# Moving the last 128 columns of each attention tile's polynomial from VectorE to GpSimd in an eight-core attention and feed-forward kernel

## The chip, the cores and the metric

One Trainium2 chip; the program runs on all 8 of its cores, with different data and the same instructions. The metric is device time in microseconds (us) of the slowest core. The engines of a core are TensorE (PE in the profile, its weight loads PEld), VectorE (DVE), ScalarE (ACT), GpSimd (POOL) and SyncE (SP, which issues most of the DMAs).

## The reference

One transformer layer on x of shape (4, 4096, 1024), float32. Cut to what matters:

```python
def polymax(x):                       # in place of a softmax
    poly = where(x > 0, x ** 2 + 1.0, 0.0)
    lin  = where((x >= -100) & (x <= 0), -0.01 * x + 1.0, 0.0)
    return (poly + lin) / 1000.0

def attn(x, W_attn, W_proj):          # 16 heads of 64, causal
    q, k, v = split(x @ W_attn)
    att = einsum('bhid,bhjd->bhij', q, k) / 8
    att = polymax(where(causal, att, -inf))
    return einsum('bhij,bhjd->bhid', att, v) @ W_proj

def ffn(x, U1, V1, b1, U2, V2, b2):   # low rank, 256
    return gelu(x @ U1 @ V1 + b1) @ U2 @ V2 + b2

x = x + attn(layernorm(x), W_attn, W_proj)
x = x + ffn(layernorm(x), U1, V1, b1, U2, V2, b2)
```

## The kernel before

**Split over cores.** Two cores share one of the four sequences. Each core computes keys and values of all 4096 positions and attention, projection and feed-forward for 2048 of them (every second tile of 128 rows). Data lie transposed: features on the 128 partitions, positions along the free dimension.

**Stages, one after the other.** (1) Layernorm of the whole sequence. (2) K, V and Q projections for the first half of the keys, and running sums of k times v (`msnap`, `prefsnap`). (3) Attention over the first half of the keys, `emit_attention(0)`. (4) K and V of the second half. (5) `emit_attention(1)`. (6) Projection, second layernorm, feed-forward, output. A bf16 score s is turned into relu(s) times (relu(s) + 0.01): with the linear part taken from the running sums, that is polymax up to constants.

**Attention, the part that is touched.** The loops are: chunk c (four query chunks of 512 columns), head pair p (8), key tile idx (up to 16 tiles of 128 keys). I call one (c, p) a sweep. One key tile of one head pair goes through five steps, in buffer `sb = idx % 3` of three:

- QK, L688 (`emit_qk`): two TensorE matmuls, one for each head, into two PSUM banks, N columns each. N is 512, but for the last six key tiles of a chunk's diagonal it is 384, 384, 256, 256, 128, 128.
- relu, L708: ScalarE reads both banks (2 x N columns) and writes `eb`. Masked tiles (eight for each chunk, those on the diagonal) have a second ScalarE operation, L713, on the first 128 columns of each head, into `zb`.
- polynomial, L721: VectorE, one SCALAR_TENSOR_TENSOR, (e + 0.01) * e, from `eb` into `gb`. Both of its tensor operands are the same `eb` tile in SBUF.
- mask, L728 and L733: VectorE, two TENSOR_TENSOR on 2 x 128 columns, for masked tiles only.
- AV, L753 (`emit_av`): two TensorE matmuls with `gb` as the moving operand, accumulating in bank 4 or 5; for masked tiles two more, L761. The first tile of a sweep adds up to eight matmuls with `msnap`, L779.

At a sweep's end VectorE copies the accumulated bank out in four pieces (L802, L806, L811 or L814).

**Order and waits.** Each engine's instructions are written out by hand in program order. TensorE starts a sweep with QK of tiles 0, 1, 2; then for each idx comes QK(idx + 3) and AV(idx). Every engine has one semaphore (T, S, V, P for TensorE, ScalarE, VectorE, GpSimd) that each of its operations raises by one. `b.wait(engine, sem, count)` makes an engine's queue wait; a wait already covered by an earlier one is dropped. QK(idx + 3) waits for ScalarE's reads of its banks (`s_rel`), the relu of idx waits until VectorE is done with `eb` of idx - 3 (`e_rel`), the polynomial waits for AV of idx - 3 (`g_rel`), and AV waits for the polynomial (`gcnt`) or for the mask (`mcnt`). `ss=True` on an operation adds a wait of the engine for its own previous operation. GpSimd issues nothing in this kernel but four memsets of constants at the start.

**How many tiles.** For each head pair there are 80 key tiles over both halves: 48 unmasked with N = 512, and for each of four chunks two masked ones of each N of 512, 384, 256 and 128. With 8 head pairs: 384 unmasked tiles of N = 512, and 64 masked tiles of each of the four sizes, 640 in all. In the first half of the keys, chunks 2 and 3 have unmasked tiles only (16 sweeps of 16 tiles).

Of the kernel before, what the change touches and what calls it, by code (L numbers as in the profile page):

```python
# [8 lines left out]
BF16 = mybir.dt.bfloat16  # L9
# [4 lines left out]
D, T, HD, NP, DC, OWNT = 1024, 4096, 64, 8, 8, 2048  # L14
# [100 lines left out]
def view(pool, byte_off, dtype, shape):  # L115
    esz = mybir.dt.size(dtype)
    assert byte_off % 32 == 0 and byte_off % esz == 0
    n = prod(shape[1:])
    ap = pool.bitcast(dtype).ap()[0:shape[0], byte_off // esz: byte_off // esz + n]
    if len(shape) > 2:  # L120
        names = [f"a{i}" for i in range(len(shape) - 1)]
        spec = "p (" + " ".join(names) + ") -> p " + " ".join(names)
        ap = ap.rearrange(spec, **{names[i]: shape[i + 1] for i in range(len(shape) - 1)})
    return ap


def build_program(upto="full", dumps=()):
# [26 lines left out]
    with contextlib.ExitStack() as stack:  # L154
# [4 lines left out]
        poolD = E_(nc.sbuf_tensor("poolD", [128, 28672], U8))  # L159
# [14 lines left out]
        b = Build(nc)  # L174
# [8 lines left out]
        def tfence():  # L183
# [31 lines left out]
        eb = view(poolD, 0, BF16, [128, 6, 512])  # L215
        gb = view(poolD, 6144, BF16, [128, 6, 512])
        ab = view(poolD, 12288, BF16, [128, 6, 512])
        zb = view(poolD, 18432, BF16, [128, 3, 2, 128])
        zmb = view(poolD, 12288, BF16, [128, 3, 2, 128])
        ktb2_ = [view(poolD, 24576, BF16, [128, 1024]),  # L220
                 view(poolD, 26624, BF16, [128, 1024])]
        wkvb = view(poolD, 0, BF16, [128, DC, 1024])
# [163 lines left out]
        for tb in range(8):  # L386
# [28 lines left out]
            for dc in range(DC):  # L415
                if dc + 2 < DC:
# [9 lines left out]
                     inc="T")  # L426
# [9 lines left out]
                 ss=True)  # L436
# [11 lines left out]
        for tb in range(8):  # L448
# [26 lines left out]
            for dc in range(DC):  # L475
                if dc + 2 < DC:
# [3 lines left out]
                                 o=lnxh[tb // 4][:, dc, (tb % 4) * 512:(tb % 4 + 1) * 512],  # L480
                                 t=tmp2[dc % 4], n=bank(bkb): e.tensor_add(o, t, n),
                                 inc="V")
# [6 lines left out]
        s_rel = [0, 0, 0]  # L489
        z_rel = [0, 0, 0]  # L490
        e_rel = [0, 0, 0]
        ab_rel = [0, 0, 0]
        zw_rel = [0, 0, 0]
        g_rel = [0, 0, 0]
# [166 lines left out]
        def emit_attention(half):  # L661
            b.wait("tensor", "V", b.cnt["V"])
            for c in range(4):
# [3 lines left out]
                for p in range(NP):  # L667
# [24 lines left out]
                    def is_m(idx):  # L692
                        return 8 * c <= kts[idx] <= 8 * c + 7

                    gcnt, mcnt = {}, {}

                    def emit_eg(idx, qkT):
                        ktg = kts[idx]
                        sb = idx % 3
                        masked = is_m(idx)  # L700
                        j0 = max(4 * c + 1, ktg // 2 + 1)
                        coloff = (j0 - (4 * c + 1)) * 128
                        N = 512 - coloff
                        b.wait("scalar", "T", qkT)
                        b.wait("scalar", "V", e_rel[sb])
                        b.op("scalar", lambda e, o=eb[:, 2 * sb:2 * sb + 2, 0:N],
                             i=ps8[:, SBK[sb]:SBK[sb] + 2, 0:N]:
                             e.activation(o, i, AF.Relu), inc="S")  # L708
                        if masked:
                            b.wait("scalar", "V", zw_rel[sb])  # L710
                            b.op("scalar", lambda e, o=zb[:, sb, :, :],
                                 i=ps8[:, SBK[sb]:SBK[sb] + 2, 0:128]:
                                 e.activation(o, i, AF.Identity, scale=-0.01,  # L713
                                              bias=consts[:, 1:2]), inc="S")
                        s_rel[sb] = b.cnt["S"]
                        b.wait("vector", "S", s_rel[sb])
                        b.wait("vector", "T", g_rel[sb])
                        gcnt[idx] = b.op("vector",
                                         lambda e, o=gb[:, 2 * sb:2 * sb + 2, 0:N],
                                         i=eb[:, 2 * sb:2 * sb + 2, 0:N]:  # L720
                                         e.scalar_tensor_tensor(o, i, 0.01, i,  # L721
                                                                ALU.add, ALU.mult),
                                         inc="V")
                        if masked:
                            midx = ktg % 2
                            zw_rel[sb] = b.op("vector", lambda e, o=zmb[:, sb, :, :],
                                              z=zb[:, sb, :, :], m=masksb[:, midx, :, :]:
                                              e.tensor_mul(o, z, m), inc="V")  # L728
                            b.wait("vector", "V", gcnt[idx])
                            mcnt[idx] = b.op("vector",  # L730
                                             lambda e, o=gb[:, 2 * sb:2 * sb + 2, 0:128],
                                             m=masksb[:, midx, :, :]:
                                             e.tensor_mul(o, o, m), inc="V")  # L733
                        e_rel[sb] = b.cnt["V"]

                    def emit_av(idx):
# [5 lines left out]
                        coloff = (j0 - (4 * c + 1)) * 128  # L742
                        N = 512 - coloff
                        b.wait("tensor", "V", mcnt[idx] if is_m(idx) else gcnt[idx])
                        if idx == 0:
                            b.wait("tensor", "V", av_free[avbk])
                        for hh in range(2):
# [432 lines left out]
```

How the kernel before makes its waits and increments, by code:

```python
        def wrapped(e, fn=fn, h=h, w=selfw):  # L60
            i = fn(e)
            if w:
                i.wait_op(h, w, "sem-ge")
            i.then_inc(h, 1)
# [3 lines left out]
    def _dma_on(self, queue, dst, src):  # L68
        key = f"dma{self.dma_n}"
        assert self.dma_n < self.N_DMA_SEMS, "DMA sem pool exhausted"
        h = self.dma_sems[self.dma_n]
        self.sem_handles[key] = h
        self.cnt[key] = 16
        self.dma_n += 1
        for e_ in self.ENGINES:
            self.last_wait[e_][key] = 0
        self.streams[queue].append(
            lambda e, d=dst, s=src, h=h: e.dma_start(out=d, in_=s).then_inc(h, 16))
        return key
# [7 lines left out]
    def wait(self, eng, sem, val):  # L87
        if not val or val <= 0:
            return
        assert val <= self.cnt[sem], f"{eng} waits future {sem}={val} (now {self.cnt[sem]})"
        if self.last_wait[eng][sem] >= val:
            return
        self.last_wait[eng][sem] = val
        h = self.sem_handles[sem]
        self.streams[eng].append(lambda e, h=h, v=val: e.wait_ge(h, v))
```

## Time and profile before

| What | us |
|---|---|
| median of 2 runs | 2118.15 (2117.35 to 2118.95) |
| the profiled execution | 2118.03 |
| its span on the slowest core (core 3) | 2116.5 |
| spans of the 8 cores | 2105.9 to 2116.5 |
| VectorE busy in the span | 1258.3 |
| TensorE matmuls busy | 1300.9 |
| ScalarE busy | 759.7 |
| GpSimd busy | 0.2 |

The span runs from the first to the last instruction of the core; 1.5 us of the execution's time lie outside it. A busy TensorE is not TensorE at its peak, since matmuls are pipelined and the clock that it is granted changes: full speed is 2.4 GHz, and 0.50 in a view is 1.2 GHz. The attention stages are two stretches: about 515 to 1113 us, and 1357 to 1620 us.

### The profile page before, as it was taken

How to read it: one execution, taken by the hardware profiler on the slowest of the kernel's cores; microseconds unless marked ns; L12 is line 12 of the kernel's file. 1: busy time of each engine (PE TensorE's matmuls, PEld its weight loads, DVE VectorE, ACT ScalarE, POOL GpSimd, SP SyncE). 2: the span in 40 equal slices, each digit the busy share in tenths (PEclk: the TensorE clock that was granted, in tenths of full speed). 3: DMA queues.
4: the chain of work that ended last, by engine and by line, in shares of the span. 5: the costliest groups of instructions: out<-in, count | busy, mean ns of one | idle time of the engine just before them, and what ended most of it. 6: DMA issues, size and time to landing. Idle time of an engine off the chain costs nothing.

```text
span 2116.5 us, 22621 instructions; the slowest of 8 cores (2105.9 to 2116.5 us)
## 1 busy us (share of the span) xinstructions
PE 1300.9 (61%) x6880; PEld 470.3 (22%) x6880; DVE 1258.3 (59%) x2171; ACT 759.7 (36%) x1074; POOL 0.2 (0%) x4
## 2 busy tenths in 40 slices
PE   3423286478667776767762747667674642478776
PEld 0001032243222221111111313322221220023332
DVE  4558433245889999999992323588996233334422
ACT  1100000001668777877770000267774000143233
POOL 0000000000000000000000000000000000000000
PEclk8755597798556667777786969755666775588898
DMA  5435201200000000000002020000001542001111
GB/s 163 159 124 194 80 20 60 80 1 1 1 1 1 1 1 1 1 1 1 1 1 79 21 60 1 1 1 1 1 1 41 166 144 86 0 0 41 40 40 40
DMA packets 37398, 87.68 MB, mean 41 GB/s; under 512 B 1953, under 2 KB 7330, under 8 KB 37282
## 3 DMA queue, kind: packets, MB, share of 16 engines
q1 hardware_dynamic: 30562, 75.75, 11.0%
q10 hardware_dynamic: 6720, 10.49, 1.7%
q8 instruction: 60, 0.98, 0.2%
q14 instruction: 56, 0.46, 0.1%
HBM read 77.85 MB, written 8.39 MB: 41 GB/s over the span
## 4 chain that ended last, share of the span: by engine, by line
PE 41%; DVE 28%; issue 16%; DMA 10%; ACT 4%; DVEq 1%; SPq 0%; ACTq 0%
DVE poolD L721 15%; DMA poolD<-W_attn 6%; PE ps L753 5%; PE ps L688 3%; PE ps L1041 3%; PE ps L864 3%; PE ps L592 3%; PE ps L955 3%; PE ps L849 3%; PE ps L612 3%; PE ps L1061 3%; PE ps L634 3%; ACT poolD L708 2%; DVE poolD L733 2%; DMA poolD<-W_proj 1%
## 5 line engine op out<-in xcount | busy, mean ns | idle before, releaser
L708 ACT ACTIVATE poolD<-ps 128x1024 bf16<-128x1024 f32 (+3 forms) x640 | 560.4, 900 | 853.0 <-PE ps L688 669.3
L721 DVE SCALAR_TENSOR_TENSOR poolD<-poolD 128x1024 bf16<-128x1024 bf16 (+3 forms) x640 | 647.8, 1059 | 44.6 <-ACT poolD L708 22.9
L753 PE MATMUL ps<-poolD,poolA 128*64 128x512 bf16 (+3 forms) x1280 | 311.6, 471 | 227.1 <-DVE poolD L721 115.8
L688 PE MATMUL ps<-poolB,poolA 64*128 64x512 bf16 (+3 forms) x1280 | 287.0, 475 | 33.8 <-ACT poolD L713 16.4
L753 PEld LDWEIGHTS ps<-poolD,poolA 128*64 128x64 bf16 x1280 | 94.0, 119 | 420.0 <-issue 420.0
L1053 ACT ACTIVATE poolC<-ps,sb_b1s 128x512 bf16<-128x512 f32 x128 | 87.4, 687 | 127.3 <-PE ps L1041 82.7
L713 ACT ACTIVATE poolD<-ps,consts 128x256 bf16<-128x256 f32 x256 | 123.8, 483 | 0.0
L688 PEld LDWEIGHTS ps<-poolB,poolA 64*128 64x128 bf16 x1280 | 64.8, 102 | 239.1 <-issue 238.0
L761 PE MATMUL ps<-poolD,poolA 128*64 128x128 bf16 x512 | 86.4, 305 | 0.0
L864 PE MATMUL ps<-poolD,poolC 128*128 128x512 bf16 x256 | 62.9, 403 | 36.9 <-DVE poolD L836 36.9
L1041 PE MATMUL ps<-poolC,poolB 128*128 128x512 bf16 x256 | 78.8, 392 | 9.6 <-DVE poolC L1029 6.2
L592 PE MATMUL ps<-poolC,poolD 128*128 128x512 bf16 x256 | 58.3, 392 | 42.0 <-DVE poolD L571 42.0
L955 PE MATMUL ps<-poolC,poolD 128*128 128x512 bf16 x256 | 58.2, 392 | 39.2 <-DVE poolD L898 39.2
L849 PE MATMUL ps<-poolC,poolD 128*128 128x512 bf16 x256 | 57.3, 388 | 37.1 <-DVE poolD L836 37.1
L364 ACT ACTIVATE poolD<-ps 1x512 f32<-1x512 f32 x4 | 2.3, 586 | 216.3 <-PE ps L360 216.3
L1061 PE MATMUL ps<-poolC,poolB 128*128 128x512 bf16 x256 | 78.7, 391 | 1.7 <-ACT poolC L1053 1.7
L358 PE MATMUL ps<-poolD,sb_onescol 128*1 128x512 bf16 x32 | 18.9, 591 | 96.6 <-DVE poolD L355 96.6
L634 PE MATMUL ps<-poolC,poolD 128*128 128x512 bf16 x256 | 59.8, 386 | 28.0 <-DVE poolD L571 27.2
L423 PE MATMUL ps<-poolD,sb_onescol 128*1 128x512 bf16 x64 | 33.6, 526 | 69.8 <-DVE poolD L420 69.7
L733 DVE TENSOR_TENSOR poolD<-poolD,sb_masksb 128x256 bf16<-128x256 bf16 x256 | 72.9, 285 | 1.0 <-DVE poolD L728 1.0
L612 PE MATMUL ps<-poolD,poolC 128*128 128x512 bf16 x256 | 56.8, 385 | 26.7 <-DVE poolD L571 26.7
L728 DVE TENSOR_TENSOR poolD<-poolD,sb_masksb 128x256 bf16<-128x256 bf16 x256 | 72.8, 284 | 0.0
(100 smaller groups left out, 1154.6 us busy)
## 6 DMA issues: line engine op xcount, KB each, us to landing
poolD<-x_t SPq DMA_DIRECT2D x8, 2048.0 KB, 9.8
poolA<-x_t SPq DMA_DIRECT2D x8, 2048.0 KB, 9.7
poolD<-W_attn SPq DMA_DIRECT2D x12, 1024.0 KB, 5.0
poolD<-W_attn SPq DMA_DIRECT2D x16, 512.0 KB, 3.6
poolC<-x_own_t SPq DMA_DIRECT2D x8, 1024.0 KB, 5.1
y<-poolC SPq DMA_DIRECT2D x4, 2048.0 KB, 6.6
poolD<-W_proj SPq DMA_DIRECT2D x8, 512.0 KB, 3.7
poolD<-U ACTq DMA_DIRECT2D x5, 512.0 KB, 4.3
```

The lines of the kernel that those rows point to most:

```text
L592: sp=(dc == DC - 1): e.matmul(o, l, r, skip_group_check=True, start=st, stop=sp), inc="T")
L634: e.matmul(o, l, r, skip_group_check=True, start=st, stop=sp), inc="T")
L688: e.matmul(o, l, r, skip_group_check=True, start=True, stop=True, tile_position=tp),
L708: e.activation(o, i, AF.Relu), inc="S")
L713: e.activation(o, i, AF.Identity, scale=-0.01, bias=consts[:, 1:2]), inc="S")
L721: e.scalar_tensor_tensor(o, i, 0.01, i, ALU.add, ALU.mult),
L753: e.matmul(o, l, r, skip_group_check=True, start=st, stop=True, tile_position=tp),
L849: e.matmul(o, l, r, skip_group_check=True, start=st, stop=sp), inc="T")
L864: e.matmul(o, l, r, skip_group_check=True, start=st, stop=sp), inc="T")
L955: e.matmul(o, l, r, skip_group_check=True, start=st, stop=sp), inc="T")
L1041: e.matmul(o, l, r, skip_group_check=True, start=st, stop=sp), inc="T")
L1061: e.matmul(o, l, r, skip_group_check=True, start=st, stop=sp), inc="T")
```

## The change

For tiles with N of 384 or 512, the last 128 columns of each head (`hi` to N, 2 x 128 elements in a partition) leave the VectorE operation. GpSimd computes them with two operations: `abh = e + 0.01` (a new buffer of 2 x 128 columns, a single one), then `gb = abh * e`. Tiles with N of 256 and 128 are as before. The relu of a tile now also waits for GpSimd's work on `eb` three tiles earlier (`e_relP`), and AV also waits for GpSimd's second operation (`pcnt`). GpSimd waits for the relu (S), for AV of three tiles before (T) and for its own operation before (`ss=True`).

```diff
+        abh = view(poolD, 13824, BF16, [128, 2, 128])
...
+        e_relP = [0, 0, 0]
...
                         b.wait("scalar", "V", e_rel[sb])
+                        b.wait("scalar", "P", e_relP[sb])
...
                         b.wait("vector", "S", s_rel[sb])
                         b.wait("vector", "T", g_rel[sb])
+                        hi = N - 128 if N >= 384 else N
                         gcnt[idx] = b.op("vector",
-                                         lambda e, o=gb[:, 2 * sb:2 * sb + 2, 0:N],
-                                         i=eb[:, 2 * sb:2 * sb + 2, 0:N]:
+                                         lambda e, o=gb[:, 2 * sb:2 * sb + 2, 0:hi],
+                                         i=eb[:, 2 * sb:2 * sb + 2, 0:hi]:
                                          e.scalar_tensor_tensor(o, i, 0.01, i,
                                                                 ALU.add, ALU.mult),
                                          inc="V")
+                        if hi < N:
+                            b.wait("gpsimd", "S", s_rel[sb])
+                            b.wait("gpsimd", "T", g_rel[sb])
+                            b.op("gpsimd", lambda e, o=abh[:, :, :],
+                                 i=eb[:, 2 * sb:2 * sb + 2, hi:N]:
+                                 e.tensor_scalar_add(o, i, 0.01), inc="P", ss=True)
+                            pcnt[idx] = b.op("gpsimd",
+                                             lambda e, o=gb[:, 2 * sb:2 * sb + 2, hi:N],
+                                             a=abh[:, :, :],
+                                             i=eb[:, 2 * sb:2 * sb + 2, hi:N]:
+                                             e.tensor_mul(o, a, i), inc="P", ss=True)
+                            e_relP[sb] = pcnt[idx]
+                        else:
+                            pcnt[idx] = 0
...
                         b.wait("tensor", "V", mcnt[idx] if is_m(idx) else gcnt[idx])
+                        b.wait("tensor", "P", pcnt[idx])
```

How the instructions stand now. On VectorE, in chunk 1 of the first half (the end of one sweep and the first tiles of the next), there stood before; a row ending in x6 is six alike:

```order
L811 TENSOR_SCALAR poolC<-ps,prefsnap 128x128 x3
L721 SCALAR_TENSOR_TENSOR poolD<-poolD 128x1024 [waits sem_S] x3
L721 SCALAR_TENSOR_TENSOR poolD<-poolD 128x1024 [waits sem_S,sem_T] x6
L728 TENSOR_TENSOR poolD<-poolD,sb_masksb 128x256
L733 TENSOR_TENSOR poolD<-poolD,sb_masksb 128x2x128 [waits sem_V]
L721 SCALAR_TENSOR_TENSOR poolD<-poolD 128x1024 [waits sem_S,sem_T]
```

The same place now (the changed file's lines 725, 746 and 751 are lines 721, 728 and 733 of before):

```order
L830 TENSOR_SCALAR poolC<-ps,prefsnap 128x128 x3
L725 SCALAR_TENSOR_TENSOR poolD<-poolD 128x2x384 [waits sem_S] x3
L725 SCALAR_TENSOR_TENSOR poolD<-poolD 128x2x384 [waits sem_S,sem_T] x6
L746 TENSOR_TENSOR poolD<-poolD,sb_masksb 128x256
L751 TENSOR_TENSOR poolD<-poolD,sb_masksb 128x2x128 [waits sem_V]
L725 SCALAR_TENSOR_TENSOR poolD<-poolD 128x2x384 [waits sem_S,sem_T]
```

VectorE has the same instructions in the same order; the polynomial has 2 x 384 elements in place of 1024. On GpSimd, which had nothing there, the attention stages now have 1024 instructions (512 pairs); a few near their start, where L733 is the addition and L738 the multiplication:

```order
L738 TENSOR_TENSOR poolD<-poolD 128x2x128 [waits sem_P]
L733 TENSOR_SCALAR poolD<-poolD 128x256 [waits sem_S,sem_P]
L738 TENSOR_TENSOR poolD<-poolD 128x2x128 [waits sem_P]
L733 TENSOR_SCALAR poolD<-poolD 128x256 [waits sem_S,sem_T,sem_P]
L738 TENSOR_TENSOR poolD<-poolD 128x2x128 [waits sem_P]
```

Each multiplication waits for the addition before it, and each addition for the multiplication before it. On TensorE, in the middle of such a sweep, there stood AV (L753) and QK (L688) in turn:

```order
L753 MATMUL ps<-poolD,poolA 64x512 [waits sem_V]
L753 MATMUL ps<-poolD,poolA 64x512
L688 MATMUL ps<-poolB,poolA 128x512 [waits sem_S]
L688 MATMUL ps<-poolB,poolA 128x512
L753 MATMUL ps<-poolD,poolA 64x512 [waits sem_V]
```

and now (L772 is AV, L690 is QK):

```order
L772 MATMUL ps<-poolD,poolA 64x512 [waits sem_V,sem_P]
L772 MATMUL ps<-poolD,poolA 64x512
L690 MATMUL ps<-poolB,poolA 128x512 [waits sem_S]
L690 MATMUL ps<-poolB,poolA 128x512
L772 MATMUL ps<-poolD,poolA 64x512 [waits sem_V,sem_P]
```

Nothing has moved on TensorE; AV has one wait more, and the QK behind it in the queue stands behind that wait too.

## Rows read from the trace of the kernel before

**Rows 1.** The page: busy time of each engine, and the span in 40 slices.
```profile
PE 1300.9 (61%) x6880; PEld 470.3 (22%) x6880; DVE 1258.3 (59%) x2171; ACT 759.7 (36%) x1074; POOL 0.2 (0%) x4
...
DVE  4558433245889999999992323588996233334422
ACT  1100000001668777877770000267774000143233
POOL 0000000000000000000000000000000000000000
```
**Rows 2.** Busy time by stretches of the attention stages, all engines.
```profile
513.00:597.00 84.00, 54.59 (x367) 19.21 (x365) 69.50 (x186) 56.73 (x110) 0.00 (x0) 0.53 0.00 1
597.00:797.00 200.00, 143.80 (x834) 45.26 (x835) 185.66 (x344) 152.12 (x226) 0.00 (x0) 0.64 0.00 1
800.00:1113.50 313.50, 219.15 (x974) 58.96 (x970) 288.05 (x304) 238.68 (x240) 0.00 (x0) 0.76 0.00 1
```
**Rows 3.** Groups of instructions by shape, 500 to 1640 us: busy, mean ns, idle before.
```profile
L721 DVE SCALAR_TENSOR_TENSOR poolD<-poolD 128x1024 bf16<-128x1024 bf16 x448 | 516.3, 1220 | 43.7 <-ACT poolD L708 22.9 <-ACT poolD L713 20.0 <-issue 0.3
L708 ACT ACTIVATE poolD<-ps 128x1024 bf16<-128x1024 f32 x448 | 443.8, 1026 | 818.8 <-PE ps L688 655.8 <-DVE poolC L802 55.3 <-DVE poolC L811 43.8
L713 ACT ACTIVATE poolD<-ps,consts 128x256 bf16<-128x256 f32 x256 | 123.8, 483 | 0.0
L728 DVE TENSOR_TENSOR poolD<-poolD,sb_masksb 128x256 bf16<-128x256 bf16 x256 | 72.8, 284 | 0.0
L721 DVE SCALAR_TENSOR_TENSOR poolD<-poolD 128x768 bf16<-128x768 bf16 x64 | 60.9, 952 | 0.2 <-ACT poolD L713 0.2
L721 DVE SCALAR_TENSOR_TENSOR poolD<-poolD 128x512 bf16<-128x512 bf16 x64 | 43.8, 685 | 0.2 <-issue 0.2
```
**Rows 4.** In order of time, unmasked tiles, TensorE at its higher clock: start, duration.
```profile
807.46 12.57 DVE L721 SCALAR_TENSOR_TENSOR poolD<-poolD 128x1024 bf16<-128x1024 bf16 x11
...
809.96 0.41 PE L753 MATMUL ps<-poolD,poolA 128*64 128x512 bf16 x2 [0.41 <-DVE poolD L721]
810.30 0.39 PE L688 MATMUL ps<-poolB,poolA 64*128 64x512 bf16 x2
...
820.93 0.89 DVE L802 CAST poolC<-ps 128x128 bf16<-128x128 f32 x4 [0.89 <-PE ps L753]
821.55 2.86 ACT L708 ACTIVATE poolD<-ps 128x1024 bf16<-128x1024 f32 x3 [3.80 <-DVE poolC L802]
822.67 2.36 DVE L721 SCALAR_TENSOR_TENSOR poolD<-poolD 128x1024 bf16<-128x1024 bf16 x2 [0.86 <-ACT poolD L708]
```
**Rows 5.** The same view at 800 us, with TensorE at its lower clock.
```profile
804.76 7.31 ACT L708 ACTIVATE poolD<-ps 128x1024 bf16<-128x1024 f32 x7 [0.33 <-PE ps L688]
805.07 0.60 PE L688 MATMUL ps<-poolB,poolA 64*128 64x512 bf16 x2
805.61 0.64 PE L753 MATMUL ps<-poolD,poolA 128*64 128x512 bf16 x2
806.18 0.61 PE L688 MATMUL ps<-poolB,poolA 64*128 64x512 bf16 x2
```
**Rows 6.** The same view, VectorE only, masked tiles of N = 512 and 384.
```profile
529.31 1.23 DVE L721 SCALAR_TENSOR_TENSOR poolD<-poolD 128x1024 bf16<-128x1024 bf16 x1 [1.04 <-ACT poolD L713]
...
530.86 1.22 DVE L721 SCALAR_TENSOR_TENSOR poolD<-poolD 128x1024 bf16<-128x1024 bf16 x1
...
532.39 0.95 DVE L721 SCALAR_TENSOR_TENSOR poolD<-poolD 128x768 bf16<-128x768 bf16 x1
...
533.67 0.95 DVE L721 SCALAR_TENSOR_TENSOR poolD<-poolD 128x768 bf16<-128x768 bf16 x1
```
**Rows 7.** Who waited for whom, 500 to 1640 us: total, times, longest.
```profile
PE ps L753 <- DVE poolD L721: 115.8, 232, 0.7
```
**Rows 8.** L721 between 800 and 1000 us: duration in ns, min/median/max.
```profile
L721 DVE SCALAR_TENSOR_TENSOR poolD<-poolD x154: 1217/1219/1227, 801.8 to 999.0; 128x1024 bf16<-128x1024 bf16 x154
```
**Rows 9.** ScalarE with 512 columns, feed-forward stage, from the page.
```profile
L1053 ACT ACTIVATE poolC<-ps,sb_b1s 128x512 bf16<-128x512 f32 x128 | 87.4, 687 | 127.3 <-PE ps L1041 82.7
```

More of the change, by code:

```diff
@@ L693, in is_m @@
                         return 8 * c <= kts[idx] <= 8 * c + 7
-                    gcnt, mcnt = {}, {}
+                    gcnt, mcnt, pcnt = {}, {}, {}
                     def emit_eg(idx, qkT):
```

## The prediction

> **What bounds the kernel now.** I read the page first. No engine is busy for more than 61% of the span, but VectorE stands at 9 tenths or close to it in the slices that are attention, and GpSimd at 0 [rows 1]. So the question is asked of the attention stages alone. The busy time by stretches confirms it: VectorE is busy 185.66 of 200 us and 288.05 of 313.5 us (93% and 92%) in chunk 1 and in chunks 2 and 3, ScalarE 76% in both [rows 2]. The rows in order of time show who waits. Between 807 and 820 us eleven polynomials stand back to back on VectorE: 12.57 us, less the last one's 1.22, over 10 gives one tile each 1.135 us. TensorE, at its higher clock, waits 0.41 us for VectorE before each AV [rows 4], in all 115.8 us for L721 [rows 7]. One polynomial lasts 1220 ns by the groups [rows 3]: about 0.085 us of it lies beside its successor. The next engines are near: ScalarE needs (7.31 - 1.03) / 6 = 1.047 us for a tile, and TensorE at its lower clock 1.11 us (QK starts 805.07 and 806.18, with AV between) [rows 5]. So VectorE has 0.09 us to give on an unmasked tile, and with TensorE at 1.2 GHz 0.03. On masked tiles of N = 512 VectorE takes 1.55 us (529.31 to 530.86) and of N = 384 1.28 us (532.39 to 533.67) [rows 6].
>
> **Part 1, what VectorE gives up.** In 448 tiles of N = 512 the polynomial falls from 1024 to 768 elements, 1220 to 952 ns; in 64 of N = 384 from 768 to 512, 952 to 685 ns [rows 3]. That is 0.268 us for each of 512 tiles, 137 us of VectorE's time. If nothing else came, ScalarE and TensorE would be late next, and of the 137 us at most some 60 would be seen (third rival).
>
> **Part 2, what GpSimd takes on.** For each of the 512 tiles two operations of 256 elements, the second waiting for the first. The trace of before has no such operation on GpSimd, so its price is bounded by the nearest rows of the same size or above. The least is VectorE's TENSOR_TENSOR of 256 elements, 284 ns; the dearest operation of 256 elements is ScalarE's L713, 483 ns [rows 3]; beyond these stand ScalarE's 512 columns, 687 ns [rows 9], and VectorE's 1024, 1220 ns [rows 3]. I take 0.483 us for each, 0.966 for the pair: an engine not built for such streams won't be quicker than the slowest that is shown at the size. Ends for the range: 0.568 and 1.374 for the pair.
>
> By the Trainium skill (GPSIMD Engine Reference, Elementwise, side-by-side cycle accounting) a two-input addition of 2048 fp32 elements takes GpSimd 4497 ns, which scaled down is an estimate of 0.56 us for 256 elements; two such would make the sum below 2598 us instead of 2519. No row here has GpSimd at such work.
>
> **Part 3, beside VectorE or in turn with it.** VectorE's polynomial, its mask products and both GpSimd operations read SBUF at the same time. Either they run side by side, so that a tile costs the slower of the two engines, or they take turns, so that it costs their sum. What the trace shows is one case of two engines on this data: ScalarE writes the next `eb` tile during each polynomial, and L721 stays at 1217 to 1227 ns over 154 of them [rows 8]. So there is no general slowing by neighbours, and nothing on GpSimd. Bounds for the interference are therefore zero and the whole duration. I take the whole: VectorE's polynomial is the only operation there that reads two operands of full width at once and runs at 1 element in 1.1 ns, while the mask product with its 256 elements in 284 ns is quicker for each, so I expect it to hold all of VectorE's ways to the memory for all of its time. This is a choice, with a chance below.
>
> The Trainium skill has a rule on just this (SBUF — State Buffer, Who interferes with whom): GpSimd's SBUF port is VectorE's second one, and a VectorE instruction with two SBUF inputs and a GpSimd instruction that reads SBUF exclude each other for a whole instruction. By that rule the sum is the one in turns, 2519 us; without it the rows allow 2070 to 2300 us.
>
> **The sum, in turns.** An unmasked tile: 0.952 + 0.966 = 1.918 us against 1.135, since the 0.085 us that VectorE's operations lie beside each other goes too when another engine stands between. That is +0.783 us. A masked tile of N = 512 has the same polynomial and the same mask work as before: +0.783. Of N = 384: 0.685 + 0.966 = 1.651 against 0.952 - 0.085 = 0.867, +0.784. So 512 x 0.783 = 401 us. What hides nothing: ScalarE's 1.047 and TensorE's 1.11 us are both below 1.918, so they are idle and their clocks don't matter there.
>
> **The waits.** AV now waits for GpSimd's second operation, and behind AV in TensorE's queue stands the QK of the tile four on, for which ScalarE waits; the relu of a tile waits for GpSimd three tiles before. From the end of a relu to the polynomial's start it takes 0.10 us (relu 821.55 + 1.03, polynomial 822.67) [rows 4]. With three buffers these hops, and the one between addition and multiplication, lie beside other tiles' work: VectorE can go on in the gap. I cost them at nothing; without cover, a hop of 0.10 on 512 tiles is 51 us. At a sweep's end the gap (AV, copy of the bank, first QK, first relu) is unchanged at 2.64 us: 820.03 to 822.67 in [rows 4]. Stages outside attention have no changed instruction. GpSimd's very first operation may cost more once; it starts after 515 us of idleness and one such is below 0.5%.
>
> Made against the profiled execution: 2118.0 (span 2116.5 and 1.5 outside) + 401 = 2519 us. The median of the runs is 2118.15, so it is the same number. With the pair at 0.568: +0.385 x 512 = +197, 2315 us. At 1.374: +1.191 x 512 = +610, 2728 us.
>
> **The rivals.**
>
> *Side by side, and GpSimd's chain is the bound.* Then a tile costs the pair and two hops of 0.10. At 0.966 that is 1.166 us, +0.03 on 384 unmasked tiles, 12 us, and 0.2 us at the end of each of the 16 sweeps whose last tile has GpSimd work, 3 us: 2133. At 1.374 it is 1.574 us: +0.44 x 384 = 169, and 10 us more at masked tiles and sweep ends: 2297. Middle value 2210 (pair 1.16). For it: L721's steadiness beside ScalarE [rows 8]. Against: nothing in the trace but that both read the same tile.
>
> *Side by side and cheap, not slower.* The place is AV's wait, the price is the pair's, and the point is 2P + 0.20 = 1.135, so P = 0.47 us an operation. Below it ScalarE or TensorE sets the tile. Unmasked: 1.135 - 1.047 = 0.09 us x 384 = 34 us with TensorE at the higher clock, 10 us at the lower. Masked: VectorE falls by 0.268, of which ScalarE and TensorE leave some 0.2: x 128 = 26 us. Together 36 to 60, 2058 to 2082 us; I name 2070. For it: VectorE's own 284 ns for 256 elements [rows 3]. Against it: it needs both a GpSimd as fast as ScalarE and no interference.
>
> *In turns and dearer than I bound it.* A GpSimd operation above 0.687 us, up to VectorE's 1.22 for 1024 elements: 0.952 + 2.44 - 1.135 = 2.257 x 512 = +1156, 3274 us at the far end. Against it: that is four times VectorE's time for an element.
>
> **How the numbers follow.** In turns (2315 to 2728, named 2519): 0.68. GpSimd's chain side by side: 0.18, of which 0.05 within 2%. Cheap side by side: 0.07, of which 0.03 below 2076. Dearer: 0.07. A measurement of this kernel tells about 2% from no change. Faster 0.03, within 2% 0.05 + 0.04 = 0.09, slower 0.68 + 0.13 + 0.07 = 0.88. The range leaves out the cheap case, the dear one and the lower part of the chain case, about 0.2: 2180 to 2760.
>
> **What would show it.** Right: in the attention stages a tile each 1.9 us or so, GpSimd's operations and VectorE's polynomial not beside each other, or those of VectorE drawn out above 952 ns in the records; AV waiting for GpSimd; ScalarE idle for about half the time; all added time between the first and the last L725, and none in the other stages. If polynomials last 952 ns and stand 0.2 us or more apart with GpSimd busy all the time, the chain rival holds. The forecast is wrong if a tile takes under 1.5 us, or if GpSimd's pair comes out under 0.57 or over 1.37 us.

## The result and the profile after

The changed kernel takes 2641.55 us (median of 12 runs, 2626.62 to 2653.76) against 2120.99 us (10 runs of the kernel before beside it). The ratio is 1.244, 95% interval 1.2403 to 1.2476: 24% slower, +521 us. The forecast was 2519 us (+401), range 2180 to 2760, with 0.88 for slower. Some executions of every kernel here show a lower granted clock on one die and take a few per cent longer: the medians hold all executions, the ratios leave those out.

The page of the changed kernel, busy time of each engine and the span in 40 slices, beside [rows 1]:

```profile
span 2638.8 us, 25581 instructions; the slowest of 8 cores (2619.4 to 2638.8 us)
PE 1416.5 (54%) x6880; PEld 488.5 (19%) x6880; DVE 1296.3 (49%) x2171; ACT 776.3 (29%) x1074; POOL 1060.3 (40%) x1028
DVE  4584333487666544454444322358666633343332
POOL 0000000156777888888888600035777710000000
PEclk8655897855555555555555577975555558557678
...
POOL 38%; PE 30%; DVE 10%; DMA 8%; issue 8%; ACT 5%; POOLq 0%; DVEq 0%; SPq 0%; ACTq 0%
```

VectorE, at 9 tenths in the attention slices before, stands at 4 to 8 now, and GpSimd at 5 to 8. GpSimd, which was not in the chain that ended last, now makes up 38% of it. VectorE's busy time did not fall by the 137 us of work that it gave up: it rose from 1258.3 to 1296.3. So VectorE is both idle for longer and slower while it works. TensorE's clock stands at 5 tenths, the 1.2 GHz level, through the attention slices; in the middle of a sweep that costs nothing, since TensorE waits there for GpSimd (below). The groups by shape, 500 to 2160 us, show the second, beside [rows 3]:

```profile
L733 POOL TENSOR_SCALAR poolD<-poolD 128x256 bf16<-128x256 bf16 x512 | 600.4, 1173 | 1018.4 <-ACT poolD L716 842.0 <-ACT poolD L711 135.8
L725 DVE SCALAR_TENSOR_TENSOR poolD<-poolD 128x768 bf16<-128x768 bf16 x448 | 478.3, 1076 | 394.6 <-ACT poolD L711 318.1 <-ACT poolD L716 55.4 <-PE ps L798 10.8
L738 POOL TENSOR_TENSOR poolD<-poolD 128x256 bf16<-128x256 bf16 x512 | 459.7, 898 | 42.8
L746 DVE TENSOR_TENSOR poolD<-poolD,sb_masksb 128x256 bf16<-128x256 bf16 x256 | 118.2, 462 | 0.0
```

768 elements take VectorE 1076 ns, where [rows 3] has 952, and the mask product 462 ns where it had 284. GpSimd's two operations last 1173 and 898 ns in the mean. Their minimum is 847 and 666 ns. In order of time, unmasked tiles (start, duration), beside [rows 4]:

```profile
949.52 0.96 DVE L725 SCALAR_TENSOR_TENSOR poolD<-poolD 128x768 bf16<-128x768 bf16 x1 [0.47 <-ACT poolD L711]
949.84 1.17 POOL L738 TENSOR_TENSOR poolD<-poolD 128x256 bf16<-128x256 bf16 x1
951.09 0.85 POOL L733 TENSOR_SCALAR poolD<-poolD 128x256 bf16<-128x256 bf16 x1
...
952.02 0.67 POOL L738 TENSOR_TENSOR poolD<-poolD 128x256 bf16<-128x256 bf16 x1
952.30 1.21 DVE L725 SCALAR_TENSOR_TENSOR poolD<-poolD 128x768 bf16<-128x768 bf16 x1 [1.81 <-ACT poolD L711]
952.78 1.44 POOL L733 TENSOR_SCALAR poolD<-poolD 128x256 bf16<-128x256 bf16 x1
...
953.98 0.96 DVE L725 SCALAR_TENSOR_TENSOR poolD<-poolD 128x768 bf16<-128x768 bf16 x1 [0.47 <-ACT poolD L711]
954.30 1.17 POOL L738 TENSOR_TENSOR poolD<-poolD 128x256 bf16<-128x256 bf16 x1
```

Two tiles take 4.46 us (949.84 to 954.30), so one takes 2.23 us against 1.135. GpSimd is never idle here for more than the 0.08 us hop between its operations. The operations that start with VectorE idle last 0.85 and 0.67 us, and those that start beside a polynomial 1.44 and 1.17 us. The multiplication that starts at 949.84 ends 0.53 us after the polynomial has (950.48), so only 0.14 of its 0.67 us lie beside it; of the 0.85 us of the addition at 952.78 it is 0.14 too (it ends at 954.22, the polynomial at 953.51). And the polynomial of 952.30, which starts while a multiplication is under way, lasts 1.21 us in place of 0.96. This pattern is the rule: in chunks 2 and 3 of the first half the additions stand 1.69 and 2.77 us apart in turn, in 211 of 252 steps. Who waited for whom, 500 to 2160 us:

```profile
PE ps L772 <- POOL poolD L738: 567.0, 496, 2.2
ACT poolD L711 <- POOL poolD L738: 522.7, 463, 1.9
```

Both waits that the diff adds are live in nearly all of the 512 tiles. The attention stages took all but some 12 us of the +522 us in the spans: from the first relu to the start of the last AV, the first one went from 596 us (515.5 to 1111.2) to 988 (511.6 to 1499.9) and the second from 262 (1356.9 to 1619.2) to 380 (1745.3 to 2125.1). With 384 and 128 tiles that GpSimd shares, that is +1.02 and +0.92 us a tile.

### The profile page after: what moved, and what is told of

The parts are those of the page before. It is cut to its first block, busy times and chain, and to the rows that moved or that the text cites. A ratio compares the mean times of both kernels' runs of the same rounds, so it can differ in the third digit from the quotient of the medians.

```text
span 2638.8 us, 25581 instructions; the slowest of 8 cores (2619.4 to 2638.8 us)
## 1 busy us (share of the span) xinstructions
PE 1416.5 (54%) x6880; PEld 488.5 (19%) x6880; DVE 1296.3 (49%) x2171; ACT 776.3 (29%) x1074; POOL 1060.3 (40%) x1028
## 3 DMA queue, kind: packets, MB, share of 16 engines
q8 instruction: 62, 1.02, 0.2%
## 4 chain that ended last, share of the span: by engine, by line
POOL 38%; PE 30%; DVE 10%; DMA 8%; issue 8%; ACT 5%; POOLq 0%; DVEq 0%; SPq 0%; ACTq 0%
POOL poolD L733 20%; POOL poolD L738 18%; DMA poolD<-W_attn 5%; ACT poolD L711 3%; PE ps L690 3%; PE ps L1060 3%; PE ps L1080 2%; PE ps L883 2%; PE ps L868 2%; PE ps L614 2%; PE ps L594 2%; PE ps L636 2%; PE ps L974 2%; PE ps L772 1%; DMA poolD<-W_proj 1%
## 5 line engine op out<-in xcount | busy, mean ns | idle before, releaser
L733 POOL TENSOR_SCALAR poolD<-poolD 128x256 bf16<-128x256 bf16 x512 | 600.4, 1173 | 1018.4 <-ACT poolD L716 842.0
L711 ACT ACTIVATE poolD<-ps 128x1024 bf16<-128x1024 f32 (+3 forms) x640 | 567.3, 897 | 1347.0 <-PE ps L690 659.7
L725 DVE SCALAR_TENSOR_TENSOR poolD<-poolD 128x768 bf16<-128x768 bf16 (+2 forms) x640 | 619.5, 974 | 455.3 <-ACT poolD L711 318.1
L772 PE MATMUL ps<-poolD,poolA 128*64 128x512 bf16 (+3 forms) x1280 | 364.1, 558 | 636.8 <-POOL poolD L738 567.0
L738 POOL TENSOR_TENSOR poolD<-poolD 128x256 bf16<-128x256 bf16 x512 | 459.7, 898 | 42.8
L690 PE MATMUL ps<-poolB,poolA 64*128 64x512 bf16 (+3 forms) x1280 | 329.7, 541 | 34.4 <-ACT poolD L711 16.7
L772 PEld LDWEIGHTS ps<-poolD,poolA 128*64 128x64 bf16 x1280 | 102.3, 130 | 873.5 <-issue 868.8
L690 PEld LDWEIGHTS ps<-poolB,poolA 64*128 64x128 bf16 x1280 | 67.1, 105 | 282.9 <-issue 281.8
L746 DVE TENSOR_TENSOR poolD<-poolD,sb_masksb 128x256 bf16<-128x256 bf16 x256 | 118.2, 462 | 0.0
L1060 PE MATMUL ps<-poolC,poolB 128*128 128x512 bf16 x256 | 85.5, 422 | 7.8 <-DVE poolC L1048 6.2
L1080 PE MATMUL ps<-poolC,poolB 128*128 128x512 bf16 x256 | 86.5, 425 | 1.5 <-ACT poolC L1072 1.4
L751 DVE TENSOR_TENSOR poolD<-poolD,sb_masksb 128x256 bf16<-128x256 bf16 x256 | 79.7, 311 | 0.8 <-DVE poolD L746 0.8
L359 PE MATMUL ps<-poolD,sb_onescol 128*1 128x512 bf16 x32 | 18.9, 590 | 95.5 <-DVE poolD L356 95.5
```

The lines of the kernel that those rows point to most:

```text
L690: e.matmul(o, l, r, skip_group_check=True, start=True, stop=True, tile_position=tp),
L725: e.scalar_tensor_tensor(o, i, 0.01, i, ALU.add, ALU.mult),
L733: e.tensor_scalar_add(o, i, 0.01), inc="P", ss=True)
L738: e.tensor_mul(o, a, i), inc="P", ss=True)
L772: e.matmul(o, l, r, skip_group_check=True, start=st, stop=True, tile_position=tp),
L1060: e.matmul(o, l, r, skip_group_check=True, start=st, stop=sp), inc="T")
```

## The experiments

Two things could make a tile 1.1 us longer: GpSimd's own time for the pair, and the two engines getting in each other's way. Runs 1 to 3, 6 and 8 take away one or the other, 4 and 5 change the size, 7 and 9 look at VectorE alone, 10 and 11 at what a use of GpSimd without the turns is worth. All ratios are to the kernel before, run beside it on the same chip.

**1. `one_op`: one GpSimd operation in place of two.**

```diff
-                            b.op("gpsimd", lambda e, o=abh[:, :, :],
-                                 i=eb[:, 2 * sb:2 * sb + 2, hi:N]:
-                                 e.tensor_scalar_add(o, i, 0.01), inc="P", ss=True)
...
-                                             a=abh[:, :, :],
+                                             a=eb[:, 2 * sb:2 * sb + 2, hi:N],
```

> GpSimd's addition is left out (the last 128 columns become e * e without the 0.01), so one GpSimd operation stands for each of the 512 tiles in place of two. Theory of turns: VectorE's 0.96 us and the multiplication exclude each other, with up to 0.14 us of GpSimd's start hidden: a tile takes 0.96 + 0.53 to 0.67 = 1.49 to 1.63 us against 1.135, so +0.36 to +0.50 us on 512 tiles, 2300 to 2375 us. Rival, no turns, GpSimd is only slow: one operation of 0.67 us and a hop of 0.08 is below ScalarE's 1.05 us, so the kernel would be as fast as before or faster, 2060 to 2120 us.

Measured: 2198.97 us, ratio 1.0373 (1.0329 to 1.0418). Seven polynomials and six products in a row:

```profile
898.91 9.07 DVE L725 SCALAR_TENSOR_TENSOR poolD<-poolD 128x768 bf16<-128x768 bf16 x7
899.53 7.63 POOL L735 TENSOR_TENSOR poolD<-poolD 128x256 bf16<-128x256 bf16 x6
```

Neither number was met. One operation of 0.61 us (the product alone, run 8) is far from filling GpSimd, yet the kernel is 78 us slower: both engines stand back to back in the records, a tile each (9.07 - 1.36) / 6 = 1.285 us, where 1.36 us is the length of one such polynomial. Undisturbed polynomials of 768 elements would be 0.867 us apart; the product adds 0.42 of its own 0.61 us. So turns there are, but a GpSimd operation of 0.61 us costs VectorE only 0.42.

**2. `memset`: GpSimd writes and reads nothing.**

```diff
-                                 e.tensor_scalar_add(o, i, 0.01), inc="P", ss=True)
+                                 e.memset(o, 0.01), inc="P", ss=True)
...
-                                             e.tensor_mul(o, a, i), inc="P", ss=True)
+                                             e.memset(o, 0.01), inc="P", ss=True)
```

> Both GpSimd operations become writes of a constant (same places written, same waits, nothing read), so the last 128 columns hold no data of the input. Theory of turns by the second read port alone: VectorE's polynomial is back at 952 ns in all records and nothing of GpSimd is drawn out; if a write costs GpSimd under 0.5 us the kernel is at 2060 to 2130 us. Rival, any GpSimd access excludes VectorE: polynomials of 1.1 to 1.4 us remain, and a tile is at least 0.95 us plus the pair, 2250 us or more.

Measured: 2035.44 us, ratio 0.9602 (0.956 to 0.9643), 4% faster than before. The groups:

```profile
L725 DVE SCALAR_TENSOR_TENSOR poolD<-poolD 128x768 bf16<-128x768 bf16 x448 | 419.7, 958 | 74.3 <-ACT poolD L711 35.2 <-ACT poolD L716 24.9 <-PE ps L770 2.4
L736 POOL MEMSET poolD<- 128x256 bf16 x512 | 159.3, 311 | 29.3
```

The polynomial is at 958 ns with GpSimd writing beside it. This run keeps every wait, every hop and 1024 GpSimd operations, and it is where the kernel would be if they cost 0.31 us each and met nobody: with the added waits in place, what VectorE gave up is still worth 85 us. ScalarE now comes near to setting the tile:

```profile
909.59 8.35 ACT L711 ACTIVATE poolD<-ps 128x1024 bf16<-128x1024 f32 x9
```

Nine relus stand back to back, 0.90 us from start to start (the last one lasts 1.13 us), where the prediction has 1.047 for ScalarE.

**3. `dve_small`: GpSimd without VectorE.**

```diff
+                        lo = 32 if N >= 384 else N
...
-                                         lambda e, o=gb[:, 2 * sb:2 * sb + 2, 0:hi],
-                                         i=eb[:, 2 * sb:2 * sb + 2, 0:hi]:
+                                         lambda e, o=gb[:, 2 * sb:2 * sb + 2, 0:lo],
+                                         i=eb[:, 2 * sb:2 * sb + 2, 0:lo]:
```

> VectorE's polynomial is cut to the first 32 columns of each head in the 512 tiles that GpSimd shares (the columns between 32 and the last 128 are left at zero or stale, two memsets are added at stage starts); GpSimd's work and all waits stay. Theory of turns: without VectorE GpSimd's chain is 0.85 + 0.67 and two hops of 0.08, 1.68 us a tile: 2118 + 0.545 x 384 + 0.14 x 64 + 0.40 x 64 = 2362 us, with the addition at 0.85 and the multiplication at 0.67 in nearly all unmasked tiles. Rival, GpSimd's pair takes 2.2 us by itself and VectorE has no part in it: unchanged, 2640 us.

Measured: 2376.74 us, ratio 1.1212 (1.1164 to 1.126), 15 us from the number of the first theory.

```profile
L737 POOL TENSOR_SCALAR poolD<-poolD x512: 847/848/1167, 524.0 to 1873.8; 128x256 bf16<-128x256 bf16 x171
```

(min/median/max in ns.) The addition takes 848 ns in the median with VectorE's polynomial nearly gone, against 1167 in the changed kernel. So GpSimd's pair is dear by itself: its chain alone makes the kernel 12% slower.

**4. `cols64`: 64 columns of each head on GpSimd.**

```diff
-                        hi = N - 128 if N >= 384 else N
+                        hi = N - 64 if N >= 384 else N
```

> GpSimd takes 64 columns of each head in place of 128, VectorE 64 more. If GpSimd's price goes by elements: chain of 0.42 + 0.34 + 0.16 = 0.92 us alone, with turns about 1.085 + 0.6 = 1.7 us a tile, some +0.55 x 512, 2400 us. If it is a fixed cost for each operation: the chain is still 1.68 us, VectorE's share 0.13 longer, 2640 to 2700 us.

Measured: 2419.04 us, ratio 1.1411 (1.123 to 1.1593), as in the case where the price goes mostly by elements. Undisturbed, the two operations have

```profile
905.78 0.53 POOL L733 TENSOR_SCALAR poolD<-poolD 128x128 bf16<-128x128 bf16 x1
...
906.39 0.43 POOL L738 TENSOR_TENSOR poolD<-poolD 128x128 bf16<-128x128 bf16 x1
```

against 0.85 and 0.67 us for twice the elements: 0.21 us fixed and 2.5 ns for each element of a partition, and 0.19 us and 1.9 ns.

**5. `cols16`: 16 columns.** The same edit with `N - 16`.

> GpSimd takes 16 columns of each head. From the measured 0.85 and 0.67 us at 128 columns and 0.53 and 0.43 at 64, an operation is about 0.2 us fixed plus 2.5 or 1.9 ns an element: 0.28 and 0.25 us at 16 columns, a chain of 0.69 us that bounds nothing. VectorE's share is 992 of 1024 elements, 1.10 us a tile, and turns add the streaming part, 0.08 + 0.06 us: 1.24 us, +0.1 on 448 tiles, about 2165 us. Rival, turns cost a whole operation: 1.10 + 0.53 = 1.63 us, 2360 us; without turns 2105 us.

Measured: 2271.61 us, ratio 1.0675 (1.0572 to 1.0779): between the two numbers and on neither. In order of time:

```profile
901.54 1.19 DVE L725 SCALAR_TENSOR_TENSOR poolD<-poolD 128x992 bf16<-128x992 bf16 x1 [1.39 <-ACT poolD L711]
901.74 1.13 POOL L733 TENSOR_SCALAR poolD<-poolD 128x32 bf16<-128x32 bf16 x1
...
902.96 0.24 POOL L738 TENSOR_TENSOR poolD<-poolD 128x32 bf16<-128x32 bf16 x1
```

An addition of 32 elements, 0.29 us alone, lasts 1.13 us and ends 0.14 us after the polynomial. GpSimd waits out the whole polynomial however little it has to do. What I had left out is this latency: AV and the relu three tiles on need both GpSimd operations, and one of them loses most of a polynomial's time. An addition that waits and a multiplication that does not come to 1.52 us a tile (1.11 in the median + 0.24 and two hops of 0.08), and that is the median distance of the additions in chunks 2 and 3, where GpSimd is idle for more than 0.2 us only at the ends of sweeps. Its own work and the hops are 0.69 us of it; the rest is waiting. Giving GpSimd less does not make the split cheap: 3% of a tile's elements cost 6.7% of the kernel's time.

**6. `psum_operand`: VectorE's second operand from PSUM.** Both GpSimd operations as in the changed kernel.

```diff
+                                         j=ps8[:, SBK[sb]:SBK[sb] + 2, 0:hi]:
-                                         e.scalar_tensor_tensor(o, i, 0.01, i,
+                                         e.scalar_tensor_tensor(o, i, 0.01, j,
                                                                 ALU.add, ALU.mult),
                                          inc="V")
+                        z_rel[sb] = gcnt[idx]
```

> Based on the changed kernel, GpSimd's two operations as they are. VectorE's polynomial takes its second operand from the score banks in PSUM instead of from eb, so that it reads SBUF only once (for negative scores it then gives 0.01 s in place of 0; QK of three tiles later waits for it). Theory, the turns come from VectorE's second SBUF operand: L725 no longer drawn out by GpSimd, GpSimd's addition and multiplication at 0.85 and 0.67 us beside it, GpSimd's chain alone sets the unmasked tile at 1.68 us, 2360 to 2400 us. Rival, any VectorE work excludes GpSimd: a tile stays at 2.2 us, 2640 us.

Measured: 2342.2 us, ratio 1.1007 (1.09 to 1.1114). The groups, and two neighbours in order of time:

```profile
L735 POOL TENSOR_SCALAR poolD<-poolD 128x256 bf16<-128x256 bf16 x512 | 435.1, 850 | 1020.3 <-ACT poolD L716 843.8 <-ACT poolD L711 135.7
L726 DVE SCALAR_TENSOR_TENSOR poolD<-poolD,ps 128x768 bf16<-128x768 bf16 x448 | 424.5, 953 | 256.3 <-ACT poolD L711 196.3 <-ACT poolD L716 37.7 <-PE ps L690 15.7
L740 POOL TENSOR_TENSOR poolD<-poolD 128x256 bf16<-128x256 bf16 x512 | 343.4, 671 | 42.9
```

```profile
899.05 0.95 DVE L726 SCALAR_TENSOR_TENSOR poolD<-poolD,ps 128x768 bf16<-128x768 bf16 x1 [0.73 <-ACT poolD L711]
899.54 0.85 POOL L735 TENSOR_SCALAR poolD<-poolD 128x256 bf16<-128x256 bf16 x1
```

Same elements, same two engines, now side by side: 953, 850 and 671 ns in the mean of all, hardly drawn out. A tile takes 1.685 us, which is 0.85 + 0.67 and two hops. This is the deciding run: the turns come from VectorE reading SBUF twice while GpSimd reads it, not from VectorE working as such, and not from both reading the same `eb` tile, which they still do here. The mask products still read SBUF twice, and the second of them is still drawn out:

```profile
L753 DVE TENSOR_TENSOR poolD<-poolD,sb_masksb 128x256 bf16<-128x256 bf16 x256 | 104.2, 407 | 1.0 <-DVE poolD L748 1.0
```

That is 407 ns against 285 before. The run also splits the loss: 2342 - 2121 = 221 us stay without the polynomial's turns (GpSimd's own time, less what VectorE gave up), and 2641 - 2342 = 299 us are those turns.

**7. `dve_two`: two VectorE operations, no GpSimd.** From the kernel before, `ab = e + 0.01`, then `gb = ab * e`, each on all N columns.

```diff
+                        acnt = b.op("vector", lambda e, o=ab[:, 2 * sb:2 * sb + 2, 0:N],
+                                    i=eb[:, 2 * sb:2 * sb + 2, 0:N]:
+                                    e.tensor_scalar_add(o, i, 0.01), inc="V")
+                        b.wait("vector", "V", acnt)
...
-                                         e.scalar_tensor_tensor(o, i, 0.01, i,
-                                                                ALU.add, ALU.mult),
+                                         e.tensor_mul(o, a, i), inc="V")
```

> Based on the kernel before, no GpSimd: the polynomial as two VectorE operations on all N columns, ab = e + 0.01, then gb = ab * e (zmb moved to other bytes). The mask product shows 256 elements of two bf16 operands in 0.20 us from start to start, so a two-operand product of 1024 should take about 0.6 us and the one-operand addition no more: if the addition goes at four elements a cycle, 0.35 + 0.60 = 0.95 us against 1.135, ScalarE's 1.05 sets the tile, 2040 to 2080 us. If the addition is no faster than the product: 1.2 us, 2130 to 2160 us. Rival, the wait between the two costs 0.2 us a tile: 2100 to 2200 us.

Measured: 2148.98 us, ratio 1.012 (1.0103 to 1.0137).

```profile
861.95 0.42 DVE L720 TENSOR_SCALAR poolD<-poolD 128x1024 bf16<-128x1024 bf16 x1
862.47 0.69 DVE L726 TENSOR_TENSOR poolD<-poolD 128x1024 bf16<-128x1024 bf16 x1
863.08 0.42 DVE L720 TENSOR_SCALAR poolD<-poolD 128x1024 bf16<-128x1024 bf16 x1
```

The addition takes 0.42 and the product 0.69 us for 1024 elements, but the wait leaves 0.10 us between the addition's end and the product, and a pair takes 1.13 us, as one operation did. That is the rival. In chunks 2 and 3 of the first half, which have no masked tile, both kernels take 328 us from the first relu to the last, so what is lost lies in the chunks with masked tiles. The run also gives the comparison for the price: VectorE adds 1024 elements in 0.42 us, GpSimd 256 in 0.85.

**8. `one_op_psum`: edits 1 and 6 together.**

> Both earlier edits together: GpSimd's addition left out (e * e in its columns) and VectorE's second operand taken from PSUM. If the turns come from VectorE's second SBUF operand and the price from GpSimd's own time, neither is left as a bound: L726 at 953 ns, GpSimd's product at 0.67 to 0.74 us beside it, ScalarE's 1.05 us or TensorE's 1.11 us sets the tile, 2040 to 2090 us. If one GpSimd operation a tile costs something of its own beyond turns (its waits, AV's wait for it), the kernel stays above 2118, up to the 2199 of the run with one operation.

Measured: 2060.27 us, ratio 0.9713 (0.9684 to 0.9742). The polynomial has 954 ns in the mean and GpSimd's product 621. With 1 and 6 and the changed kernel it makes a table of four:

| | second operand in SBUF | in PSUM |
|---|---|---|
| two GpSimd operations | 2641.55 | 2342.2 |
| one | 2198.97 | 2060.27 |

Taking away the turns is worth 299 us with two operations and 139 with one. Taking away the addition is worth 443 us with turns and 282 without.

**9. `dve_pipe`: the addition of tile k+1 ahead of the product of tile k.** As 7, with the loop

```diff
+                    emit_eg(0, fences[0])
                     for idx in range(nk):
-                        emit_eg(idx, fences[idx])
+                        if idx + 1 < nk:
+                            emit_eg(idx + 1, fences[idx + 1])
+                        emit_g(idx)
```

> The two-operation polynomial on VectorE alone, with the addition of tile k+1 issued ahead of the product of tile k, so that no operation follows directly the one it waits for. The two stood 0.525 and 0.61 us apart; the wait's part of that is 0.525 - (0.421 - 0.085) = 0.19 us. Without it 0.95 us a tile, below ScalarE's 1.05: 2050 to 2090 us. Rival, the product of a tile now waits for the relu of the next, which with three buffers holds ScalarE back: no gain, 2110 to 2150 us.

Measured: 2209.98 us, median of four runs (2186.69 to 2246.9), no interval for the ratio. Even the lowest is 3% slower than the kernel before, slower than 7, and slower than the rival's numbers too.

```profile
906.03 0.43 DVE L719 TENSOR_SCALAR poolD<-poolD 128x1024 bf16<-128x1024 bf16 x1 [0.66 <-ACT poolD L708]
...
906.37 0.69 DVE L733 TENSOR_TENSOR poolD<-poolD 128x1024 bf16<-128x1024 bf16 x1
```

The gap between the two is gone (0.34 us from start to start where it was 0.52), but VectorE now waits 0.66 us for the relu of the next tile before it may issue the product of this one. The mechanism is the rival's; its size was underestimated.

**10. `psum_only`: the PSUM operand in the kernel before.** (s + 0.01) * relu(s), with s read from PSUM, equals (relu(s) + 0.01) * relu(s).

```diff
-                                         e.scalar_tensor_tensor(o, i, 0.01, i,
+                                         e.scalar_tensor_tensor(o, j, 0.01, i,
...
+                        z_rel[sb] = gcnt[idx]
```

> Based on the kernel before, no GpSimd: the polynomial as (s + 0.01) * relu(s), with s read from PSUM, which is the same value as before. It is a control for the PSUM operand alone. A polynomial of 768 elements lasted 953 ns with it as without, so 1.135 us a tile stays, 2118 us within 1%. If QK's wait for it costs something: up to 2150 us; if the PSUM operand by itself is worth something, below 2100 us.

Measured: 2128.15 us, ratio 1.0017 (0.9995 to 1.0038). The operand alone changes nothing, so what runs 6 and 8 gained is not its doing.

**11. `psum_48`: the same operand, 48 columns of each head on GpSimd.** The changed kernel with the operand of 10 and `hi = N - 48`.

> The same operand, and GpSimd's two operations on 48 columns of each head, all values as in the reference. GpSimd alone: 0.21 + 96 x 2.5 ns = 0.45, 0.19 + 96 x 1.9 ns = 0.37, two hops of 0.08, a chain of 0.98 us; VectorE 928 elements, 0.867 + 160 / 0.96 ns = 1.03 us. Both are below ScalarE's 1.05 and TensorE's 1.11: if no turns are left the kernel gains the 0.03 to 0.09 us on 384 tiles and some on masked ones, 2055 to 2095 us. Rival, what is left of the turns (GpSimd's operations against the mask products, which read SBUF twice) and the chain eat it: 2100 to 2130 us.

Measured: 2109.09 us, ratio 0.9877 (0.9828 to 0.9926): 1.2% faster than before, below the 2% that one run tells, but clear of 1 over its runs, and with every value of the reference computed. It is the only version here that beats both kernels and leaves nothing out. The three executions that the ratio rests on took 2097.2 to 2097.5 us, 2 us over the upper end of the first expectation and below the rival's numbers.

```profile
905.93 0.45 POOL L735 TENSOR_SCALAR poolD<-poolD 128x96 bf16<-128x96 bf16 x1 [0.21 <-POOL poolD L740]
906.06 0.61 PE L690 MATMUL ps<-poolB,poolA 64*128 64x512 bf16 x2
906.46 0.36 POOL L740 TENSOR_TENSOR poolD<-poolD 128x96 bf16<-128x96 bf16 x1
906.60 0.64 PE L774 MATMUL ps<-poolD,poolA 128*64 128x512 bf16 x2
907.04 0.45 POOL L735 TENSOR_SCALAR poolD<-poolD 128x96 bf16<-128x96 bf16 x1 [0.21 <-POOL poolD L740]
907.17 0.60 PE L690 MATMUL ps<-poolB,poolA 64*128 64x512 bf16 x2
...
910.48 7.31 DVE L726 SCALAR_TENSOR_TENSOR poolD<-ps,poolD 128x928 bf16<-128x928 f32 x7
```

GpSimd's operations have the 0.45 and 0.37 us worked out from run 4. A tile takes 1.11 us here (905.93 to 907.04), which TensorE sets at its lower clock [rows 5]: its QK and AV stand back to back. Once the clock has risen, the polynomials of 928 elements do, and one tile takes (7.31 - 1.11) / 6 = 1.03 us, as expected. QK, which now waits for the polynomial, stands idle for 108 us in all; in these two stretches that sets nothing.

## Why the prediction was right, and where its sizes were off

**What bounds the kernel: right.** Run 2 shows it from the other side. With the waits kept and the polynomials of N = 512 cut by a quarter, 85 us were gained; I had allowed some 60. The room was taken too small: I read 1.047 us a tile for ScalarE from a row of seven relus [rows 5]. Idle times of about 0.1 us don't break such a row, and four of the seven begin after one of 0.08 to 0.10 us, so the number holds the pace of other engines. Back to back the relus are 0.90 us apart (run 2).

**Beside or in turn (part 3): right in kind, and the reason given was half right.** I expected VectorE's polynomial to hold all of its ways to the memory since it reads two operands. Runs 2 and 6 show that: reads of GpSimd against the second SBUF operand of VectorE, nothing else. The rule of the Trainium skill (SBUF — State Buffer, Who interferes with whom) says just this, reads only and two SBUF inputs only, and three of its cases agree with runs here: the mask product drawn out from 284 to 462 ns, the writes of run 2 that left the polynomial at 958 ns, and the PSUM operand of run 6 at 953. My other argument, that a low rate is a sign of it, is refuted: in run 6 the polynomial is as slow for an element as ever and shuts GpSimd out no longer, while the mask product, quick for each element, takes turns.

**GpSimd's price (part 2): the term that was mis-sized.** I took 0.483 us an operation, the slowest shown of 256 elements. Measured alone they are 0.85 and 0.67 us, 1.52 for the pair, above the 1.374 that I had called the high end, so the bound by rows of other engines was none. Even the estimate by the Trainium skill (GPSIMD Engine Reference, Elementwise, side-by-side cycle accounting), 0.56 us, was below; its 4497 ns for 2048 elements are 2.2 ns each, near the measured 1.9 ns of the product. What a proportion leaves out is the fixed 0.19 us; the addition, at 0.21 us and 2.5 ns, is dearer than the estimate in both.

**The sum (in turns): right in kind, too large in form.** I added whole durations: 0.952 + the pair. With the measured pair that would be 2.47 us a tile and +684 us. Measured is 2.23, and the trace of the changed kernel shows of what. In the middle of a sweep GpSimd is never idle, and a tile there is its pair (1.52), two hops (0.16) and the time in which one of its operations waits out a polynomial: 1.17 - 0.67 = 0.50 and 1.44 - 0.85 = 0.59 us in the two tiles, 0.55 in the mean, of the polynomial's 0.95. The rest of the polynomial lies beside the hops, beside the 0.14 us with which a GpSimd operation starts undisturbed, and beside the end of an addition (953.98 to 954.22, with the polynomial at its 0.96 us). So the price was 0.55 us too low in a tile and the form 0.24 us too high. That the two have opposite signs is luck: with the true price my sum would have said 2118 + 684 = 2802 us, outside the range. As it is, 120 of the 521 us were missed.

**The waits at nothing: wrong.** I let the hops lie beside other tiles' work. With the short operations of run 2 they do. In the changed kernel and in run 6 GpSimd itself sets the tile, and its two hops of 0.08 us stand in the chain: 0.16 us a tile, up to 82 us over 512 tiles, a part of the 2.23 and of the 1.685 us. In run 5 the latency of two operations in turn is most of the loss. My 0.783 us for each of 512 tiles, in all, was measured as 1.02 and 0.92 in the two stages.

**The rivals.** The chain case, side by side, is what the kernel would be without turns. Its form, the pair and two hops, is exact: 0.85 + 0.67 + 0.16 = 1.68 us against 1.685 in run 6. With the true price it gives 2342, not my 2133 to 2297. The cheap case is run 8 (2060; I had named 2070), reached only with half the work and without turns. Run 11, where 0.45 and 0.37 us gain 1.2%, agrees with its break-even of 0.47 us an operation, but does not test it: TensorE and VectorE set the tile there. The dearer case has its pair (above 1.374 us) and not its time.

**The signs.** Predicted were tiles of 1.9 us, polynomials over 952 ns, AV waiting for GpSimd, ScalarE idle for half the time and no loss elsewhere. All are in the trace but the first, which is 2.23. The sign "the forecast is wrong if the pair is over 1.37 us" fired too: the time was inside the range with the price outside its own.

What stays open: why the addition, with one operand, is slower on GpSimd (2.5 ns an element) than the product with two (1.9), and why the first 0.14 us of a GpSimd operation are free of the turn. That they are shows in every size: a product of 0.61 us ends 0.47 us after the polynomial that it met (run 1), one of 0.43 us 0.28 after (run 4), an addition of 0.29 us 0.14 to 0.15 after (run 5).

## What to carry to other kernels

Before work moves to an idle engine, price it on that engine: a run with one such operation off the critical path costs little, and rows of other engines don't bound it. Then ask which of the operations that will stand beside it read SBUF twice; where they do, count the sum and not the larger, and give even a tiny operation almost a whole neighbour's length of latency. Where one of the two operands is still in PSUM, reading it from there removes that operation's turns, at no cost here (run 10).

## What the runs showed of the hardware

- A VectorE operation with two SBUF operands and a GpSimd operation that reads SBUF exclude each other (1.44 us for 0.85; 1.21 for 0.96), but for the first 0.14 us of the GpSimd operation; with one of the operands in PSUM (953 ns, 850 and 671 ns) or with GpSimd only writing (958 and 311 ns) they run side by side.
- GpSimd, bf16, elements in a partition: addition of a constant 0.29, 0.53, 0.85 us for 32, 128, 256; product of two 0.24, 0.43, 0.67 us; a constant written to 256, 0.31 us. VectorE needs 0.42 and 0.69 us for 1024.
- A GpSimd operation of 32 elements that meets a polynomial of 1.19 us lasts 1.13 us and is done 0.14 us after it.
- VectorE's addition and product in two operations move 1024 elements in the time of the single fused one (1.13 us), 0.10 us of it the wait between them.
